# The third 16-bit part of the odd supersteps' messages, made on GpSimd instead of VectorE

## The reference, cut to what matters

```python
mask = jnp.clip(gate * (ZETA - GAMMA) + GAMMA, 0.0, 1.0)[:, 0]
rowsum = jax.ops.segment_sum(mask, row, num_segments=N_NODES) + EPS_DEG
d_inv_sqrt = jnp.clip(rowsum ** (-0.5), 0.0, 10.0)
vals = mask * d_inv_sqrt[row] * d_inv_sqrt[col]
msg = vals[:, None] * f2
return jax.ops.segment_sum(msg, row, num_segments=N_NODES)
```

## Time and profile before

| what | value |
|---|---|
| median of 3 runs | 5892.25 us (5885.24 to 5893.28) |
| the profiled execution | 5890.85 us, span 5889.1 us |
| supersteps in the two message stages | 312 |

### The profile page before, as it was taken

How to read it: one execution, slowest core, us unless ns; L and a number is a source line. 1 busy time by engine, 2 the same in 40 slices (tenths; PEclk the granted TensorE clock), 3 DMA queues, 4 the chain that set the end, 5 groups by cost and what they waited for, 6 DMA issues and landing times. The chain is left out here.

```text
span 5889.1 us, 162768 instructions
## 1 busy us (share of the span) xinstructions
PE 4101.6 (70%) x56330; PEld 3657.5 (62%) x56330; DVE 5129.1 (87%) x10832; ACT 2500.9 (42%) x5126; POOL 1164.4 (20%) x1562
## 2 busy tenths in 40 slices
PE   2777777777677888854555477888888725554777
PEld 2666666666445888854444477658888624443676
DVE  8999999999644999989999899509999799999888
ACT  2666666566044555524555200135555325554000
POOL 0000000000000333310000277303333200000776
PEclk9777677777555555556777799755555567777999
DMA  3000000000043666748999799517666579997999
GB/s 73 0 0 0 0 0 0 0 0 0 1 22 130 232 231 233 235 139 305 329 331 330 291 379 378 199 53 233 230 233 230 164 253 330 330 330 281 381 381 348
DMA packets 428687, 1120.74 MB, mean 190 GB/s; under 512 B 206962, under 2 KB 212707, under 8 KB 428023
## 3 DMA queue, kind: packets, MB, share of 16 engines
q1 hardware_dynamic: 316700, 549.97, 29.8%
q0 software_dynamic: 65856, 316.89, 14.2%
q10 hardware_dynamic: 46036, 252.74, 11.3%
HBM read 873.65 MB, written 279.36 MB: 196 GB/s over the span
## 5 line engine op out<-in xcount | busy, mean ns | idle before, releaser
L1611 PE MATMUL psG<-y_window,area 128*128 128x64 bf16 x14976 | 668.2, 217 | 780.4 <-DVE area L1256 665.3
L1611 PEld LDWEIGHTS psG<-y_window,area 128*128 128x128 bf16 x14976 | 624.7, 114 | 824.2 <-issue 504.0
L642 ACT ACTIVATE work<-iota,work 128x149 bf16<-128x149 f32 x2496 | 789.0, 406 | 0.0
L1430 PE MATMUL psG<-area,work 128*128 128x112 bf16 x2496 | 551.1, 390 | 335.4 <-DVE area L978 335.4
L586 POOL DMA_INDIRECT work<-msg_d,widx x396 | 428.3, 1082 | 1655.7 <-issue 1610.4
L1430 PEld LDWEIGHTS psG<-area,work 128*128 128x128 bf16 x2496 | 357.7, 149 | 483.7 <-issue 338.0
L1423 PE MATMUL psG<-work,merge 128*128 128x148 bf16 x4992 | 546.2, 294 | 68.9 <-ACT work L642 68.9
L1624 PE MATMUL psG<-work,edge 128*128 128x192 bf16 x4752 | 447.7, 251 | 202.8 <-DVE edge L1291 202.8
L1423 PEld LDWEIGHTS psG<-work,merge 128*128 128x128 bf16 x4992 | 529.6, 132 | 91.4 <-issue 65.6
L816 ACT ACTIVATE work<-merge 128x1024 bf16<-128x1024 f32 x312 | 330.1, 1058 | 549.4 <-DVE merge L1266 549.4
L1624 PEld LDWEIGHTS psG<-work,edge 128*128 128x128 bf16 x4752 | 412.2, 145 | 238.0 <-DVE edge L1291 163.4
(11 more groups left out here) (268 smaller groups left out, 8280.4 us busy)
## 6 DMA issues: line engine op xcount, KB each, us to landing
msg_d<-work ACTq DMA_DIRECT2D x312, 776.0 KB, 4.5
area<-rlo_d SPq DMA_DIRECT2D x312, 512.0 KB, 4.1
merge<-crel_d SPq DMA_DIRECT2D x312, 512.0 KB, 5.0
area<-crelp_d SPq DMA_DIRECT2D x312, 512.0 KB, 5.6
y_window<-y_d SPq DMA_DIRECT2D x312, 48.0 KB, 3.5
y_d<-cur SPq DMA_DIRECT2D x7, 1008.0 KB, 3.8
y_d<-work SPq DMA_DIRECT2D x7, 1008.0 KB, 4.8
work<-msg_d,widx POOLq DMA_INDIRECT x396, 6.9
```

The lines of the kernel that those rows point to most:

```text
L642: ins = act.activation(below[:, h, k, :], iota_all[:, :], ACT.Sign, bias=keyf[:, bass.ds(t * CT + k, 1)], scale=-1.0)
L1430: ins = pe.matmul(psG[:, 2 + h, 0:RECS * CT], place[:, h, :, k], spread_rec[:, h, :, :, k], start=k == 0, stop=k == CT - 1)
L1611: ins = pe.matmul(psG[:, 2 * h + k // CH, k % CH * D:(k % CH + 1) * D], col_one_hots[:, h, k * P:(k + 1) * P], y_window[:, h, m * D:(m + 1 ...
```

## The change

For odd t the third part is made by GpSimd, with the same subtraction on the same shapes, and it counts on a semaphore of its own. For even t it stays on VectorE. The waits that looked at the one semaphore look at the one of their parity. VectorE's `last_part(T - 1, 3)` after the loop goes, since superstep 155 is odd.

```diff
+        odd_third_part = sem("odd_third_part")
...
+                def odd_last_part(i):
+                    for u in (1, 3):
+                        pool.wait_ge(second_part, L * T + i * 4 + u + 1)
+                        pool.nop(nofuse=True)
+                        pool.tensor_tensor(staged[:, u, :, 2 * D:MW], scaled[:, 1, :, :], staged[:, u, :, D:2 * D], ALU.subtract).then_inc(odd_third_part, 1)
                 with pool.If(is_local):
+                    steps(pool, 0, T // 4, odd_last_part)
...
                 def store_messages(t, u):
-                    act.wait_ge(third_part, L * T + t + 1)
+                    act.wait_ge((third_part, odd_third_part)[u % 2], (L * T + t - u % 2) // 2 + 1)
...
                 def scale(t, h):
                     dve.wait_ge(y_taken, L * T + t + 1)
-                    wait(dve, third_part, L * T + t - 1)
+                    wait(dve, (third_part, odd_third_part)[h], (L * T + t - h) // 2)
...
                         scale(t, u % 2)
-                        if u > 0 or not isinstance(i, int) or i > 0:
-                            last_part(t - 1, (u - 1) % 4)
+                        if u % 2 == 1:
+                            last_part(t - 1, u - 1)
                         if not last or u < 2:
                             col_hots(i * 2 + u // 2 + 1, u % 2)
                         first_rest(t, u)
...
                     steps(dve, 0, T // 4, messages_local)
-                    last_part(T - 1, 3)
```

## The result

| what | before | after |
|---|---|---|
| median | 5892.25 us | 6001.04 us (3 runs, 5997.94 to 6003.28) |
| the profiled execution | 5890.85 us, span 5889.1 us | 6001.04 us, span 5999.3 us |

The ratio is 1.0186, with an interval of 1.0166 to 1.0206: 109 us slower, where 170 were forecast.

What follows compares the result with a forecast made beforehand. VectorE was taken to set the message stage's pace, the DMAs close behind. A pair was 3.02 + H (2.2) + 4.14 = 9.36 us, 1.08 over 8.28; with 2 us at layer ends, +170 us gave 6061 us, range 5870 to 6190.

Steps and rivals of the forecast that it cites:

- The mechanism: Message stage: GpSimd's begun subtraction keeps VectorE's two-SBUF-input operations out until it ends, holding rest(even) 3.47 to 5.22 us; chance 0.70.
- the small spread against it: Mask stage: VectorE's L1141 spreads only 735 to 749 ns beside 32-column GpSimd steps, evidence against VectorE being held.
- The order of events: In a pair: GpSimd ready at 2.48 us, hots ends at 3.02, GpSimd goes first until 5.22, then VectorE's rest(even).
- H: Time from the end of hots until GpSimd's subtraction is done: estimated 2.2 us, ends 0.93 and 3.2.
- The two prices: GpSimd's subtraction: 1.16 ns a column for one stream plus 0.94 for the second input, 2.15 us for 1024 columns.
- At the old distances, 4.14 us: VectorE behind the held rest(even): rest, scale(odd), last(even), hots to rest(odd) keep their old spacing, 4.14 us.
- 105 us is the whole prize: With GpSimd costing nothing, a pair of supersteps falls 0.67 us from 8.28, at most 105 us over 156 pairs.
- The DMAs need 0.92 x 8.28 = 7.62: First message stage: the DMA engines, taken 92%, need 7.62 us of each 8.28 us pair.
- Fall to 0.92 x 8.28 / 9.36 = 81%: Message stage: the DMA share falls to 81% as the pair grows to 9.36 us; counted at nothing.
- H below 1.12 us: Second rival: turns hold but GpSimd's operation is short, so the kernel gains, down to 5861 us; chance 0.06.
- GpSimd missing the gap: Third rival: GpSimd wakes too late for the 0.45 us behind hots; 2.00 us more per pair, 6205 us; chance 0.07.
- the first rival: VectorE is not held and GpSimd runs beside it; the pair gains 0.09 us, 5879 us in total; chance 0.17.

Runs made afterwards that it cites:

- the sixteenth: Changed kernel with GpSimd's subtraction cut to 64 of 1024 columns, the rest of odd third parts left zero: 5884.82 us, 0.9992 of the kernel before.
- the half: Changed kernel with GpSimd's subtraction cut to 512 of 1024 columns, the rest of odd third parts left zero: 5871.96 us, 0.9968 of the kernel before.

## Why the prediction was right, and where its sizes were off

- **The mechanism held.** Rest is held, by GpSimd's reading operation and not by a wait: four buffers leave it at 2.46 us, a write-only operation at 1.22. That GpSimd, once begun, keeps VectorE out was inferred from the reverse; the small spread against it fits steps too short to tell, as I had put it: the sixteenth's 64 columns lengthen hots to at most 0.89 us. The Trainium skill ("SBUF — State Buffer", section "SBUF: two separate sides") has the lock in both directions, for a VectorE operation with two SBUF inputs only against a GpSimd operation that reads SBUF, and leaves out VectorE operations with at most one SBUF input outside its 2-port performance modes. The traces agree: rest takes 2.46 us beside the subtraction and 1.22 beside the operation that only writes, and scale 1.21 beside the subtraction.
- **The order of events held**: in the pair shown GpSimd starts 0.14 us after ScalarE's second part (2994.52 + 1.06 to 2995.72; 0.17 was taken), gets the gap behind hots, and the pair follows the layout: 3.01 to the end of hots (3.02 forecast), then H, then rest to rest. By the trace 123 of the 156 rests(even) are long, in the median by 1.24 us, where 1.8 were forecast.
- **The term that was mis-sized is H**, "an estimate of H = 2.2 us". It measured 1.94 in the pair shown. Undisturbed the operation takes 2.05 us, not 2.15 and handing over, and about 0.11 of that passes while it waits for hots. The two prices, 1.16 and 0.94 ns a column, were together too much: 1.8 is measured. It seems to be the first, from an IOTA of 2384 columns, that was too high, since the experiments' IOTA of 1640 took 1.50 us, 0.91 ns a column. The Trainium skill's 2.6 cycles an element at 1.2 GHz ("GPSIMD Engine Reference", section 3.1) make an estimate of 2.2 us for 1024 columns; the measured 2.05 decides.
- **"At the old distances, 4.14 us"** was too long as well: a held rest is followed by scale 1.00 us after its release (2998.21 to 2999.21), not 1.13. Its start too is paid while it waits. Summed up: 3.01 + 1.94 + 1.00 + 3.01 = 8.96 us instead of 9.36, and 156 x (8.96 - 8.28) + 2 = 108 us, against 109 measured. Not all pairs are alike: in 30 of 156, a late load lets GpSimd hold hots instead of rest; the mean of all pairs is 8.96 us even so.
- **"105 us is the whole prize" was wrong**, though the forecast did not rest on it. "The DMAs need 0.92 x 8.28 = 7.62" took the share of a window that held the stage's ends, and read a share below 1 as room. In the middle it is 0.94 at 330 GB/s, and no kernel with the full loads got past 0.95 and 334: the sixteenth's interval takes in no change, and the same kernel with 256 KB less a superstep is 92 us faster. Had GpSimd cost next to nothing, this change would have brought 7 us by the sixteenth, which is within the noise, or 19 by the half. "Fall to 0.92 x 8.28 / 9.36 = 81%" was off as well, at 0.88: the pair is 8.96 us and not 9.36, which by the same sum gives 0.85, and the share fell less than the rate (0.92 to 0.88, 322 to 300 GB/s).
- **Rivals.** VectorE held or not: decided by rest at 2.46 us. H below 1.12 us: 1.94. GpSimd missing the gap: it did not. The price of the first rival was summed wrongly: 2.48 already holds the 0.17, so the operation would have ended at 4.63 and not 4.80, the pair would have gained 0.26 us, and the time would have been 5852 us, below the range that was drawn from 5879. Half of the columns have their GpSimd time, 1.11 us, at the break-even of 1.12, and ended 19 us faster than before, at 334 GB/s. Why half is 13 us faster than a sixteenth stays open.

Open, too, is what sets the 330 GB/s: the bytes, the number and shape of the transfers, or the two buffers of the windows. Halving the column load made each transfer smaller as well, no kernel changed the shapes at equal bytes, and none had more buffers for the windows.

## What to carry to other kernels

Before moving an elementwise operation to GpSimd, list which VectorE operations will run beside it: the ones here that read two inputs from SBUF, and the wide comparison, were held until it ended, while the one with an input in PSUM was not, so a semaphore that sets GpSimd's start decided over 87 us with the work unchanged. Price the prize with the DMA rate in the middle of the stage, and find out by loading less, and by loading earlier, whether a share of 0.94 is room or the limit. Where two engines take turns, a late load changes who is first, and one late operation then holds all behind it.

## What was not expected of the hardware

- No kernel with the full loads got past a DMA share of 0.95 and 334 GB/s in the middle of the stage, and deeper loading of the column numbers moved VectorE's wait from hots to scale.
- A waiting GpSimd operation got its turn ahead of VectorE's next operation that stood ready behind the running one, which the forecast had left open: hots took 1611 ns in the median of 312, in place of 0.75 us.
- A held operation has its start behind it: rest ended 1.07 us after the release instead of taking 1.22, and GpSimd 1.94 instead of 2.05.
- A GpSimd operation that only writes held no rest, as its own expectation had it, but collided with the wide comparison: 1.98 us in place of 1.50.
